# Every second load of a chunk split into 112, 8 and 8 partitions, in a hexagonal convolution with group norm

## The chip, the cores and the metric

The kernel runs on one core of a Trainium2 chip. The metric is the device time of one execution in microseconds. Three runs of the kernel before gave 752.25, 753.97 and 754.43 us; the median is 753.97 us. The profile is that of one more execution.

## The reference

`x` has shape (2048, 64, 16, 16) in float32: images, channels, rows, columns. What is computed is `x + conv(norm(x))`:

```
def _gn(v, G=32, eps=1e-5):           # pairs of channels of one image
    g = v.reshape(B_, G, C_ // G, H_, W_)
    return ((g - mean(g)) / sqrt(var(g) + eps)).reshape(v.shape)
...
xp = pad(x, 1); xp[:, :, DST_R, DST_C] = xp[:, :, SRC_R, SRC_C]      # 30 wrapped border pixels
up, left, right = conv4x4(xp, w_* masked to 5 taps, stride 2) + b_*
out[0::2, 0::2] = up; out[1::2, 0::2] = left; out[1::2, 1::2] = right
return x + out * OUT_MASK
```

## The kernel before

The 2048 images are taken in 64 chunks of 32 (`NCHUNK`). A chunk stands in SBUF as 128 partitions (64 channels of the even images, 64 of the odd ones) of 16 images of 256 pixels, 16 KB per partition, 2 MB in all. `xs` has eight slots for chunks (`SLOTS`); chunk k is in slot k modulo 8. It is loaded there, added to in place and stored from there.

What each engine does with chunk k:

- SP issues all transfers from one queue, in an order written out by hand (lines 177 to 209). The first chunk comes in four pieces (L179), then come the weights (L182, 64 partitions of 4 KB each), loads of chunks 1 and 2 (L169), six tiny biases (L188) and further loads up to chunk 6. After that it alternates: the store of chunk k (L175), which waits for `bank_added`, then the load of chunk k + 7 (L169), which waits until the store of chunk k - 1, which had the same slot, has landed (`stored`).
- DVE computes the statistics of chunk k + 1 (`bn`, L224, eight instructions) between the small steps that turn those of chunk k into a scale and a shift (L232 to L267), and then normalises eight of the 16 images into `tn` (L272). Before the first `bn` of a chunk it waits for the semaphore `loaded` of the slot (L221).
- ACT takes the square root (L305), normalises the other eight images (L311) and copies the finished PSUM banks of chunk k - 2 to `res`, with the bias (L340).
- POOL adds `res` to the slot (L395) and copies the wrapped border pixels in `tn` (L406).
- PE does the five taps of each of the three kernels as matmuls on 64 x 64 quarters (L451).

A load of 128 partitions is spread over 16 transfer engines, and `loaded[s]` rises by 16 when all have finished. A load's rows are 1 KB (one image of one channel), so it has 2048 of them.

Of the kernel before, what the change touches and what calls it, by code (L numbers as in the profile page):

```python
# [13 lines left out]
P = 128  # L14
B, C, HW = 2048, 64, 16
PIX = HW * HW
G = 16
NCHUNK = B // (2 * G)
SLOTS = 8
# [42 lines left out]


QUARTER = G // 4


WRAPS = [
# [14 lines left out]
def view(tensor, at, dims, first=0, parts=P):  # L82

    full = tensor[:, ]
    row = full.ap[0][0]
    return bass.AP(full.tensor, full.offset + first * row + at, [[row, parts]] + [list(d) for d in dims])


def hex_conv(nc, x, w_up, b_up, w_left, b_left, w_right, b_right, out):
    ctx = ExitStack()  # L90
    with ctx:
        def sb(name, shape, dt):
            return ctx.enter_context(nc.sbuf_tensor(name, shape, dt))

        def sem(name):
            return ctx.enter_context(nc.semaphore(name))

        x_dram = x.rearrange("(n g h) c r q -> n (h c) g (r q)", g=G, h=2)
        out_dram = out.rearrange("(n g h) c r q -> n (h c) g (r q)", g=G, h=2)

        xs = sb("xs", [P, SLOTS, G * PIX], F32)
# [26 lines left out]
        loaded = [sem(f"loaded{s}") for s in range(SLOTS)]  # L128
# [36 lines left out]
        @block.sync  # L165
        def _(sp):
            def load(k):
                s = k % SLOTS
                sp.dma_start(xs[:, s, :].rearrange("p (g q) -> p g q", g=G), x_dram[k]).then_inc(loaded[s], 16)  # L169

            def store(k):

                s = k % SLOTS
                sp.wait_ge(bank_added, NB * (k + 1))
                sp.dma_start(out_dram[k], xs[:, s, :].rearrange("p (g q) -> p g q", g=G)).then_inc(stored[s], 16)  # L175

            for n in range(4):
                pairs = slice(QUARTER * n, QUARTER * (n + 1))
                sp.dma_start(xs[:, 0, :].rearrange("p (g q) -> p g q", g=G)[:, pairs],  # L179
                             x_dram[0][:, pairs]).then_inc(quarter[n] if n < 3 else loaded[0], 16)  # L180
            for t, w in enumerate((w_up, w_left, w_right)):
                sp.dma_start(raw[:, t * C * 16:(t + 1) * C * 16],  # L182
                             w.rearrange("o c a b -> o (c a b)")).then_inc(w_loaded, 16)
            load(1)
            load(2)
            for t, b in enumerate((b_up, b_left, b_right)):
                for h in range(2):
                    sp.dma_start(bias[C * h:C * h + C, t:t + 1],  # L188
                                 b.rearrange("(o a) -> o a", a=1)).then_inc(b_loaded, 16)

            for k in range(3, SLOTS - 2):
                load(k)

            sp.wait_ge(bank_empty, PREP_BANKS)
            load(SLOTS - 2)

            for k in range(NCHUNK - 1):
                store(k)
                if k == 0:
                    load(SLOTS - 1)  # L200
                elif k + SLOTS - 1 < NCHUNK:
                    sp.wait_ge(stored[(k - 1) % SLOTS], 16 * ((k - 1) // SLOTS + 1))
                    load(k + SLOTS - 1)
            for half in range(2):
                pairs = slice(G // 2 * half, G // 2 * (half + 1))
                sp.wait_ge(bank_added, NB * (NCHUNK + half))
                sp.dma_start(out_dram[NCHUNK - 1][:, pairs],
                             xs[:, SLOTS - 1, :].rearrange("p (g q) -> p g q", g=G)[:, pairs]
                             ).then_inc(stored[SLOTS - 1], 16)
            for s in range(SLOTS):  # L210
                sp.wait_ge(stored[s], 16 * (NCHUNK // SLOTS + (s == SLOTS - 1)))

        @block.vector
        def _(dve):
            def bn(k, u0, u1):

                if k >= NCHUNK:
                    return
                s = k % SLOTS
                if u0 == 0 and k:  # L220
                    dve.wait_ge(loaded[s], 16 * (k // SLOTS + 1))  # L221
                for u in range(u0, u1):
                    both = view(xs, (s * G + 2 * u) * PIX, [(1, PIX), (PIX, 2)])
                    last = nc.vector.bn_stats(stats[:, k % 2, 2 * u:2 * u + 2].rearrange("p g a -> p (g a)"), both)  # L224
                if u1 == G // 2:
                    last.then_inc(bn_done, 1)

            def moments(k, ahead):

                done = STAT_OPS * k  # L230
                own = stats[:, k % 2]
                nc.vector.stream_shuffle(mate[:].rearrange("p g a -> p (g a)"), own.rearrange("p g a -> p (g a)"),  # L232
                                         [p ^ 1 for p in range(32)]).then_inc(stat_step, 1)
                bn(ahead, 0, 1)
                dve.wait_ge(stat_step, done + 1)
                nc.vector.tensor_tensor(gap[:], own[:, :, 1], mate[:, :, 1], ALU.subtract).then_inc(stat_step, 1)  # L236
                nc.vector.tensor_tensor(m2[:], own[:, :, 2], mate[:, :, 2], ALU.add).then_inc(stat_step, 1)  # L237
                nc.vector.tensor_tensor(msum[:], own[:, :, 1], mate[:, :, 1], ALU.add).then_inc(stat_step, 1)  # L238
                dve.wait_ge(stat_step, done + 2)
                nc.vector.scalar_tensor_tensor(gap2[:], gap[:], float(PIX // 2), gap[:],  # L240
                                               op0=ALU.mult, op1=ALU.mult).then_inc(stat_step, 1)
                bn(ahead, 1, 2)
                dve.wait_ge(stat_step, done + 5)

                nc.vector.scalar_tensor_tensor(var[:], gap2[:], EPS * GROUP, m2[:],  # L245
                                               op0=ALU.add, op1=ALU.add).then_inc(var_ready, 1)
                bn(ahead, 2, 4)
# [33 lines left out]
            for n in range(4):  # L281
                if n < 3:
                    dve.wait_ge(quarter[n], 16)
                else:
                    dve.wait_ge(loaded[0], 16)
                bn(0, QUARTER // 2 * n, QUARTER // 2 * (n + 1))
            dve.wait_ge(bn_done, 1)
# [222 lines left out]
```

## Time and profile before

| | |
|---|---|
| median of three runs | 753.97 us |
| lowest, highest | 752.25, 754.43 us |
| the profiled execution, its own time | 753.31 us |
| its span | 751.4 us |
| mean granted clock of TensorE | 0.991 |
| moved by the transfer engines | 269.68 MB, mean 359 GB/s |
| read from and written to HBM | 135.01 MB, 134.22 MB |

The span is the time from the first to the last instruction of the profile. An engine's busy share counts its instructions, without those that issue transfers or wait. The DMA share is the sum of the times of all packets over 16 engines' time; packets overlap a little on an engine, so it can stand above 1. The page's chain goes back from the last instruction, at each step to what released it.

### The profile page before, as it was taken

How to read it: one execution, taken by the hardware profiler on the slowest of the kernel's cores; microseconds unless marked ns; L12 is line 12 of the kernel's file. 1: busy time of each engine (PE TensorE's matmuls, PEld its weight loads, DVE VectorE, ACT ScalarE, POOL GpSimd, SP SyncE). 2: the span in 40 equal slices, each digit the busy share in tenths (PEclk: the TensorE clock that was granted, in tenths of full speed). 3: DMA queues.
4: the chain of work that ended last, by engine and by line, in shares of the span. 5: the costliest groups of instructions: out<-in, count | busy, mean ns of one | idle time of the engine just before them, and what ended most of it. 6: DMA issues, size and time to landing. Idle time of an engine off the chain costs nothing.

```text
span 751.4 us, 36371 instructions
## 1 busy us (share of the span) xinstructions
PE 662.4 (88%) x15697; PEld 610.1 (81%) x15697; DVE 668.0 (89%) x1793; ACT 579.5 (77%) x1258; POOL 488.1 (65%) x1115
## 2 busy tenths in 40 slices
PE   0889999999998898898898898898898898898874
PEld 0879999999998787887787887887887887887874
DVE  4899999999989999999989999999999999999910
ACT  1678889888887787787787787787787787787863
POOL 1077777777667667667667577577577676677673
PEclk9999999999999999999999999999999999999997
DMA  9999999999999999999999999999999999999984
GB/s 240 326 358 374 380 376 378 371 367 365 354 372 372 367 377 371 374 380 363 373 361 376 371 377 372 366 379 365 372 375 368 376 374 376 367 379 370 360 297 136
DMA packets 265022, 269.68 MB, mean 359 GB/s; under 512 B 2640, under 2 KB 264784, under 8 KB 264976
## 3 DMA queue, kind: packets, MB, share of 16 engines
q1 hardware_dynamic: 264976, 269.23, 104.6%
q14 instruction: 37, 0.30, 0.1%
q8 instruction: 9, 0.15, 0.1%
HBM read 135.01 MB, written 134.22 MB: 358 GB/s over the span
## 4 chain that ended last, share of the span: by engine, by line
DMA 66%; DVE 19%; PE 5%; ACT 3%; issue 3%; POOL 2%; SPq 1%; POOLq 0%; ACTq 0%
DMA xs<-in_x 41%; DMA out<-xs 25%; DVE stats L224 9%; DVE tn L272 5%; PE bank L451 5%; ACT tn L311 2%; POOL xs L395 2%; ACT res L340 1%; DVE small L256 1%; DVE small L260 1%; SPq L175 1%; DVE rstd L263 1%; POOL tn L406 1%; DVE nmr L267 1%; DVE m L237 0%
## 5 line engine op out<-in xcount | busy, mean ns | idle before, releaser
L451 PE MATMUL bank<-tn,wts 64*64 64x192 f32 (+5 forms) x15600 | 649.8, 323 | 9.1 <-issue 9.1
L451 PEld LDWEIGHTS bank<-tn,wts 64*64 64x64 f32 x15600 | 597.0, 137 | 42.3 <-issue 9.7
L395 POOL TENSOR_TENSOR xs<-res,xs 128x192 f32<-128x192 f32 (+6 forms) x780 | 388.5, 538 | 78.2 <-ACT res L340 77.7
L224 DVE BATCH_NORM_STATS2 stats<-xs 128x6 f32<-128x512 f32 x512 | 346.9, 690 | 45.4 <-DMA xs<-in_x 45.4
L340 ACT ACTIVATE res<-bank,bias 64x512 f32<-64x512 f32 (+6 forms) x650 | 304.6, 469 | 30.4 <-PE bank L451 20.6
L311 ACT ACTIVATE tn<-xs,nmr,rstd 128x256 f32<-128x256 f32 x511 | 258.9, 591 | 8.2 <-DVE nmr L267 6.7
L406 POOL COPY tn<-tn 128x128 f32<-128x128 f32 (+2 forms) x320 | 97.5, 360 | 179.5 <-ACT tn L311 179.5
L272 DVE TENSOR_SCALAR tn<-xs,rstd,nmr 128x256 f32<-128x256 f32 x513 | 198.6, 457 | 2.3
L305 ACT ACTIVATE std<-var 128x16 f32<-128x16 f32 x64 | 13.8, 215 | 123.8 <-DVE var L245 123.8
L462 PEld LDWEIGHTS bank<-blank 128*128 128x128 f16 x65 | 6.2, 96 | 70.5 <-issue 65.9
L462 PE MATMUL bank<-blank 128*128 128x2 f16 x65 | 11.4, 176 | 51.6 <-POOL tn L406 50.7
L256 DVE SCALAR_TENSOR_TENSOR small<-var,small 128x16 f32<-128x16 f32 x64 | 30.0, 468 | 0.1
L263 DVE SCALAR_TENSOR_TENSOR rstd<-small 128x16 f32<-128x16 f32 x64 | 28.5, 445 | 0.1
L430 PE MATMUL bank<-ident,xs 64*128 64x64 f32 x32 | 7.1, 419 | 19.9 <-ACT xs L353 19.9
L430 PEld LDWEIGHTS bank<-ident,xs 64*128 64x128 f32 x32 | 6.9, 329 | 19.9 <-ACT xs L353 19.9
L267 DVE SCALAR_TENSOR_TENSOR nmr<-msum,rstd 128x16 f32<-128x16 f32 x64 | 22.7, 354 | 0.1
L237 DVE TENSOR_TENSOR m<-stats,mate 128x16 f32<-128x16 f32 x64 | 21.2, 331 | 0.0
L238 DVE TENSOR_TENSOR msum<-stats,mate 128x16 f32<-128x16 f32 x64 | 19.8, 310 | 0.0
L240 DVE SCALAR_TENSOR_TENSOR gap<-gap 128x16 f32<-128x16 f32 x64 | 16.2, 252 | 0.0
L260 DVE TENSOR_TENSOR small<-small 128x16 f32<-128x16 f32 x64 | 15.7, 245 | 0.1
L253 DVE RECIPROCAL small<-std 128x16 f32<-128x16 f32 x64 | 14.8, 231 | 0.7 <-ACT std L305 0.7
L236 DVE TENSOR_TENSOR gap<-stats,mate 128x16 f32<-128x16 f32 x64 | 13.5, 211 | 0.1
(18 smaller groups left out, 36.3 us busy)
## 6 DMA issues: line engine op xcount, KB each, us to landing
xs<-in_x SPq DMA_DIRECT2D x63, 2048.0 KB, 16.8
out<-xs SPq DMA_DIRECT2D x63, 2048.0 KB, 17.0
xs<-in_x SPq DMA_DIRECT2D x4, 512.0 KB, 6.4
out<-xs SPq DMA_DIRECT2D x2, 1024.0 KB, 5.2
xs<-in_L_conv_w_up SPq DMA_DIRECT2D x1, 256.0 KB, 8.4
xs<-in_L_conv_w_left SPq DMA_DIRECT2D x1, 256.0 KB, 9.3
xs<-in_L_conv_w_right SPq DMA_DIRECT2D x1, 256.0 KB, 12.6
bias<-in_L_conv_b_up SPq DMA_DIRECT2D x2, 0.2 KB, 7.3
```

Of the source, the lines that this page charges most:

```text
L224: last = nc.vector.bn_stats(stats[:, k % 2, 2 * u:2 * u + 2].rearrange("p g a -> p (g a)"), both)
L237: nc.vector.tensor_tensor(m2[:], own[:, :, 2], mate[:, :, 2], ALU.add).then_inc(stat_step, 1)
L256: nc.vector.scalar_tensor_tensor(small[:, 1], var[:], -0.5 / GROUP, small[:, 0], op0=ALU.mult, op1=ALU.mult).then_inc(stat_step, 1)
L260: nc.vector.tensor_tensor(small[:, 2], small[:, 1], small[:, 0], ALU.mult).then_inc(stat_step, 1)
L263: nc.vector.scalar_tensor_tensor(rstd[:], small[:, 2], 1.5, small[:, 0], op0=ALU.add, op1=ALU.mult).then_inc(stat_step, 1)
L267: nc.vector.scalar_tensor_tensor(nmr[:], msum[:], -0.5, rstd[:], op0=ALU.mult, op1=ALU.mult).then_inc(norm_ready, 1)
L272: last = nc.vector.tensor_scalar(t_image(b, g), x_image(s, g), rstd[:, g:g + 1], nmr[:, g:g + 1], ALU.mult, ALU.add)
L311: last = nc.scalar.activation(t_image(k % 2, g), x_image(k % SLOTS, g), ACT.Identity, bias=nmr[:, g:g + 1], scale=rstd[:, g:g + 1])
L340: last = nc.scalar.activation(res[onto, BANK_AT[j] + at:BANK_AT[j] + at + cols], psum[NB * b + j][banks, at:at + cols], ACT.Identity, bias ...
L395: last = nc.gpsimd.tensor_tensor(onto, view(res, at, [(rows * w, pairs), (w, rows), (1, w)]), onto, ALU.add)
L406: last = nc.gpsimd.tensor_copy(view(tn[b], dst, [(T_PAIR, G)] + [(d, n) for d, _, n in dims]), view(tn[b], src, [(T_PAIR, G)] + [(d, n) fo ...
L451: last = nc.tensor.matmul(psum[bank + j][to:to + C, at:at + cols], wts[first:first + C, NT * rect[0] + n, :], taps(b, rect, tap, g0, pairs ...
```

## The change

Loads into the odd slots (1, 3, 5 and 7, so those of the odd chunks) are issued as three transfers: partitions 0 to 111, 112 to 119 and 120 to 127. By its author's count the first gives seven partitions to each of the 16 transfer engines, and each of the other two gives one to each of the lower eight, so that the lower eight carry nine partitions and the upper eight seven. All three raise the slot's semaphore by 16, and DVE waits for three times 16 there. Loads into even slots, the first chunk and all stores are unchanged.

```diff
 QUARTER = G // 4
+SPLIT = (((0, P),), ((0, 112), (112, 120), (120, P)))
...
             def load(k):
                 s = k % SLOTS
-                sp.dma_start(xs[:, s, :].rearrange("p (g q) -> p g q", g=G), x_dram[k]).then_inc(loaded[s], 16)
+                for p0, p1 in SPLIT[s % 2]:
+                    sp.dma_start(xs[p0:p1, s, :].rearrange("p (g q) -> p g q", g=G),
+                                 x_dram[k][p0:p1]).then_inc(loaded[s], 16)
...
                 if u0 == 0 and k:
-                    dve.wait_ge(loaded[s], 16 * (k // SLOTS + 1))
+                    dve.wait_ge(loaded[s], 16 * len(SPLIT[s % 2]) * (k // SLOTS + 1))
```

SP's queue around the first loads that follow a store, before the change (a row is a run of like instructions; `out<-xs` is a store, `xs<-in_x` a load, with partitions x images x pixels):

```order
L175 DMA out<-xs 128x16x256 [waits bank_added]
L169 DMA xs<-in_x 128x16x256
L175 DMA out<-xs 128x16x256 [waits bank_added]
L169 DMA xs<-in_x 128x16x256 [waits stored0]
L175 DMA out<-xs 128x16x256 [waits bank_added]
L169 DMA xs<-in_x 128x16x256 [waits stored1]
```

The same place with the change:

```order
L178 DMA out<-xs 128x16x256 [waits bank_added]
L171 DMA xs<-in_x 112x16x256
L171 DMA xs<-in_x 8x16x256 x2
L178 DMA out<-xs 128x16x256 [waits bank_added]
L171 DMA xs<-in_x 128x16x256 [waits stored0]
L178 DMA out<-xs 128x16x256 [waits bank_added]
L171 DMA xs<-in_x 112x16x256 [waits stored1]
L171 DMA xs<-in_x 8x16x256 x2
```

The loads of chunks 7 and 9 have become three issues each, the one of chunk 8 between them is as it was, and the order of chunks and waits is the same. The order of the other engines is unchanged.

## Rows read from the trace of the kernel before

**Rows 1.** The page, part 2: the span in 40 equal slices.

```profile
DMA  9999999999999999999999999999999999999984
GB/s 240 326 358 374 380 376 378 371 367 365 354 372 372 367 377 371 374 380 363 373 361 376 371 377 372 366 379 365 372 375 368 376 374 376 367 379 370 360 297 136
```

**Rows 2.** The page, parts 1 and 5: busy us and share; DVE's wait.

```profile
PE 662.4 (88%) x15697; PEld 610.1 (81%) x15697; DVE 668.0 (89%) x1793; ACT 579.5 (77%) x1258; POOL 488.1 (65%) x1115
...
L224 DVE BATCH_NORM_STATS2 stats<-xs 128x6 f32<-128x512 f32 x512 | 346.9, 690 | 45.4 <-DMA xs<-in_x 45.4
```

**Rows 3.** The page, part 4: the chain that ended last, by engine.

```profile
DMA 66%; DVE 19%; PE 5%; ACT 3%; issue 3%; POOL 2%; SPq 1%; POOLq 0%; ACTq 0%
```

**Rows 4.** The chain in order of time, middle: start us, us, what.

```profile
303.84 16.93 DMA out<-xs
320.78 16.74 DMA xs<-in_x
337.89 16.87 DMA out<-xs
354.77 16.76 DMA xs<-in_x
```

**Rows 5.** Timeline of SP, 378 to 406 us: start us, us, instruction.

```profile
378.11 5.43 SPq L169 DMA_DIRECT2D xs<-in_x  x1
383.59 5.45 SPq L175 DMA_DIRECT2D out<-xs  x1
389.09 5.71 SPq L169 DMA_DIRECT2D xs<-in_x  x1
394.85 5.31 SPq L175 DMA_DIRECT2D out<-xs  x1
400.24 5.54 SPq L169 DMA_DIRECT2D xs<-in_x  x1
```

**Rows 6.** Windows: length, busy us by engine, then PEclk, DMA share, GB/s.

```profile
65.00:110.00 45.00, 45.00 (x1064) 41.45 (x1058) 44.85 (x122) 39.91 (x87) 32.98 (x75) 1.00 1.09 378
110.00:187.00 77.00, 77.00 (x1858) 70.82 (x1854) 76.75 (x213) 67.27 (x144) 57.02 (x130) 1.00 1.07 370
188.00:278.00 90.00, 83.79 (x1995) 77.63 (x1991) 83.65 (x228) 71.84 (x155) 61.30 (x138) 1.00 1.07 368
278.00:368.00 90.00, 81.18 (x1932) 74.41 (x1928) 84.71 (x224) 70.81 (x152) 60.12 (x137) 1.00 1.07 372
548.00:638.00 90.00, 80.92 (x1927) 74.43 (x1922) 84.61 (x225) 70.96 (x152) 60.41 (x137) 1.00 1.07 374
```

**Rows 7.** The page, part 6: issues, KB each, us to landing.

```profile
xs<-in_x SPq DMA_DIRECT2D x63, 2048.0 KB, 16.8
out<-xs SPq DMA_DIRECT2D x63, 2048.0 KB, 17.0
```

**Rows 8.** The chain in order of time, early: first and last of eleven like pieces.

```profile
75.49 3.39 DVE tn L272 x8
...
178.33 2.85 DVE tn L272 x8
```

**Rows 9.** Timeline of SP, 2 to 16 us: the issues of the weights.

```profile
2.88 0.55 SPq L182 DMA_DIRECT2D xs<-in_L_conv_w_up  x1
3.47 0.63 SPq L182 DMA_DIRECT2D xs<-in_L_conv_w_left  x1
4.14 0.60 SPq L182 DMA_DIRECT2D xs<-in_L_conv_w_right  x1
```

**Rows 10.** Windows of 1 us around the weights' transfers, columns as in rows 6.

```profile
3.00:4.00 1.00, 0.00 (x0) 0.00 (x0) 0.00 (x0) 0.20 (x1) 0.27 (x2) 1.00 1.08 380
...
10.00:11.00 1.00, 0.00 (x0) 0.00 (x0) 0.86 (x2) 0.00 (x0) 0.00 (x0) 1.00 1.02 182
11.00:12.00 1.00, 0.00 (x0) 0.00 (x0) 0.43 (x1) 0.00 (x0) 0.00 (x0) 1.00 1.02 184
12.00:13.00 1.00, 0.00 (x0) 0.00 (x0) 0.00 (x0) 0.00 (x0) 0.00 (x0) 1.00 1.07 186
...
18.00:19.00 1.00, 0.00 (x0) 0.00 (x0) 1.00 (x5) 1.00 (x7) 0.00 (x0) 1.00 1.11 350
```

## The prediction

> **What bounds the kernel now.** I began with the 40 slices of the page. The DMA row stands at nine tenths in 38 of 40 slices, while no compute engine is full [rows 1]: PE is busy for 88% of the span, DVE for 89%, ACT for 77%, POOL for 65% [rows 2]. The chain that ended last puts 66% of the span on transfers and 19% on DVE [rows 3]. In the chain's middle part one load or store follows the other, each some 16.8 us from issue to landing [rows 4].
>
> That landing time isn't the cost of a transfer, for several are in flight. The cost shows in SP's own rows: SP is held 5.3 to 5.7 us in each issue, load and store alike, because the queue takes the next only as room comes free [rows 5]. The windows say the same: from 188 to 706 us the engines move 368 to 374 GB/s at a DMA share of 1.07 [rows 6]. A chunk is 128 x 4096 x 4 B = 2.10 MB, so a transfer costs 2.10 MB / 372 GB/s = **5.64 us**, and a chunk (a load and a store) 11.3 us. There are 63 loads and 63 stores of this size [rows 7], and the first chunk and the last store in pieces: 128 x 5.64 = 722 us of a span of 751.4 us.
>
> DVE is the next limit. Between 75.49 and 178.33 us, where chunks wait ready in the eight slots, the chain runs on DVE and ten chunks take 102.8 us, so 10.3 us each [rows 8]. Even there the transfers run at 370 to 378 GB/s [rows 6]. So whatever lengthens a transfer on its busiest engine lengthens the kernel, and DVE's 1 us a chunk is the most that faster transfers could give back. Afterwards DVE waits for loads 45.4 us in all [rows 2].
>
> **The change, part by part.** All durations are of one profiled execution, which took 753.31 us (span 751.4); the median of the runs shown is 753.97, so the sum is made on 753.31 and differs from the median by 0.1%.
>
> *SP's issues.* 32 of the 63 large loads (odd chunks, 1 to 63) become three issues. The 64 added ones cost SP about 0.6 us each, by the issues of the weights, the nearest ones into a queue that is not yet full [rows 9]: 38 us in all. I cost them at nothing: SP stands 5.5 us in each issue because the transfers are slow, and its issues run ahead of the data by 16.8 - 5.6 = 11 us. If that cover went, it would be 1.2 us for every second chunk. What stands behind the longer load on SP is the next store, and behind it the next load; both only fill the queue.
>
> *DVE's wait.* It waits for 48 instead of 16 in the odd slots. It costs nothing itself, but it now ends with the last of three transfers, thus with the lower eight transfer engines. Behind it on DVE stand the statistics, then the normalisation, then PE.
>
> *The share of each engine.* A whole load is eight partitions per engine in 5.64 us, so 0.705 us per partition (16 rows of 1 KB). The upper eight now have seven: 4.94 us. The lower eight have 7 + 1 + 1: were each partition as cheap as now, 6.35 us. Over a load and a store of both kinds the lower eight have 33 partitions for 32, the upper eight 31.
>
> *The two small pieces.* Here the price is open. The trace has only three transfers that reach less than 128 partitions and are not tiny: the weights, 64 partitions each. While they move, the rate falls to 182 to 186 GB/s, and the DMA share stays at 1.02 to 1.07; the whole loads around them run at 350 to 380 GB/s [rows 10]. So all engines are busy, and every packet takes 1.9 times as long. My reading: the way into the partitions of SBUF is what is shared, and with half of the partitions two engines press on the same entry. The small pieces are a sixteenth of the partitions for eight engines. Bounds: factor f = 1 (no such sharing at this size) to f = 8 (all eight engines behind one entry). In between, f = 2 is what the 64 partitions show, and f = 4 is two entries for eight engines, if neighbouring partitions lie behind the same one. I take 4, midway in doublings between the measured 2 and the worst 8, since eight neighbours are much narrower than 64.
>
> The Trainium skill, SBUF — State Buffer, section "Door 1: The DMA port swizzle", speaks against this change: four neighbouring partitions share one of 16 ports, and it gives 27.6 GB/s for partitions 0 to 3 alone. By that the eight partitions of a piece reach two ports, an estimate of 131 KB / 55.2 GB/s = 2.4 us a piece, and the sum would end near 883 us. The trace agrees as far as it goes: 64 partitions gave 183 of 350 GB/s.
>
> *Sum.* On the lower eight a split load takes 7 x 0.705 + 2 x f x 0.705 us. Against 5.64 that adds (2f - 1) x 0.705: with f = 4, 4.94 us. The stores and the even loads stay as they are. All of it lies on the path, since the transfers are the bound from end to end; it is added 32 times: 158 us. 753.3 + 158 = **911 us**. A pair of chunks takes 27.5 us instead of 22.6, DVE needs 20.6 of them.
>
> *What I leave out of the sum.* Cut by seven, the 112 partitions no longer fall on the engines in groups of eight, so neighbours behind one entry may belong to two engines. If two of an engine's seven partitions collide at double price, it adds 1.41 x 32 = 45 us. Against that, engines that drift apart don't press on the entry at once. I let the two cancel and keep both for the range.
>
> **The rivals.**
> - *f = 2 instead of 4*, since the eight engines get out of step or the entries are finer: (2 x 2 - 1) x 0.705 x 32 = 68 us, so 821 us. For it: it is the only factor measured. Against: eight engines start the pieces together, each with one partition.
> - *f = 8, one entry for all*: 15 x 0.705 x 32 = 338 us, 1092 us. For it: rate in proportion to partitions is one reading of 64 of 128. Against: it needs all eight neighbours behind one entry.
> - *No sharing, and an engine of the lower eight is the one that is late today*: it gets 33/32 of the work, 5.64 / 32 = 0.176 us for each of 128 transfers, 22.6 us: 776 us. For it: one slow engine holds the queue, and every whole transfer has the same share for each. Against: the rows of the weights.
> - *Faster: no sharing, and the engines that are late today are all in the upper eight.* Then 31/32 of their work is worth up to 22.6 us. The price is limited by the lower eight: they must move 33/32 in less than 5.64 us, thus do 5.64 x 32/33 = 5.47 us for today's share, a rate of 383 GB/s. The best slice of the page shows 380 GB/s, 5.52 us [rows 1]. From 383 GB/s on this rival decides; halfway to its 22.6 us it gives 743 us. For it: between 65 and 110 us the queue ran at 378 GB/s, later at 372, so something falls behind later. Against: the rows name no engine, and the small pieces must be free of the cost above. On this the Trainium skill, DMA: Bandwidth & Descriptors, section "Latency and other measured facts", says that engines 7 and 15 are usually the slow ones, one of each half, though for another issue path. By it the lower one would bind and the time be that of the rival before; no row here shows it.
> - *Nothing changes*: an engine's share is no limit because the memory is. Then 753 us. Against: the rate rises to 378 to 380 in stretches.
>
> **How the numbers follow.** Forecast f = 4: 0.55. f = 2: 0.18. f = 8: 0.05. No sharing, lower engine late: 0.08. Faster rival: 0.10. Nothing: 0.04. The predicted time is that of the likeliest, 911 us; its own range is 830 (much of the pressing lost by drift, half of the 158 us) to 956 (with the 45 us). The range of the whole goes down to 770, so that f = 2 (821) and the late lower engine (776) are in it, and up to 970, the 956 with a little room. It leaves out the faster rival, the unchanged case and f = 8, 0.19 in all. About 0.3% is what a measurement of this kernel can tell from no change. Faster by more: 0.10. Within: 0.04, which I round up to 0.05. Slower: 0.85.
>
> **What the profile of the changed kernel would show.** If I am right: the windows of the middle fall from 372 to about 300 GB/s, with a DMA share that falls less than the rate, because packets of the small pieces take several times as long; the time from issue to landing of the 8-partition loads is far over that of their 16 rows; DVE's wait for loads grows from 45 to over 150 us; PE and DVE keep their busy times. If the no-sharing readings hold, the rate stays within 3% of 372 GB/s. I'm wrong in kind if the rate in the middle stays at 370 or above, and wrong in size only if it falls to 340 (f = 2) or under 260 (f = 8).

## The result and the profile after

The changed kernel takes **846.33 us** (843.21 to 849.38, four runs) against 753.24 us for the kernel before in the same comparison: a ratio of **1.124** (95% interval 1.121 to 1.128), so 93 us more. Forecast were 911 us, within 770 to 970. The direction and the place are right, the size is 59% of the forecast one, and the experiments show that one term of the sum was far too large and another was left out. Where the runs of one kernel lie over 1.5% apart, the slower ones are left out of its time and ratio below.

The page after, parts 1, 2, 4 and 5, in the lines that answer to [rows 1 to 3]:

```profile
PE 701.8 (83%) x15697; PEld 636.4 (75%) x15697; DVE 647.4 (76%) x1793; ACT 579.9 (68%) x1258; POOL 488.4 (58%) x1115
...
DMA  9999999999999999999999999999999999999985
GB/s 215 226 216 304 330 347 320 327 329 336 333 343 329 323 321 336 333 351 333 328 315 335 324 356 339 319 321 340 328 348 328 327 322 333 329 343 342 321 286 196
...
DMA 55%; SPq 17%; DVE 11%; POOL 8%; PE 3%; ACT 3%; issue 2%; ACTq 0%; POOLq 0%
...
L227 DVE BATCH_NORM_STATS2 stats<-xs 128x6 f32<-128x512 f32 x512 | 347.1, 691 | 162.3 <-DMA xs<-in_x 162.1
```

The transfer engines are as full as before and move less. DVE waits 162 us for loads, where it waited 45. Of the windows, the whole middle first, then nine single microseconds around one split load (columns as in [rows 6]):

```profile
188.00:638.00 450.00, 384.84 (x8548) 347.74 (x8546) 362.89 (x1002) 317.30 (x679) 270.15 (x606) 0.92 1.06 332
...
408.00:409.00 1.00, 1.00 (x28) 0.76 (x24) 1.00 (x3) 0.96 (x4) 1.00 (x4) 1.00 1.12 210
409.00:410.00 1.00, 1.00 (x30) 0.99 (x25) 0.96 (x4) 0.97 (x3) 1.00 (x4) 1.00 1.10 205
410.00:411.00 1.00, 1.00 (x32) 0.99 (x28) 1.00 (x4) 1.00 (x3) 1.00 (x3) 1.00 1.12 205
411.00:412.00 1.00, 1.00 (x36) 1.00 (x31) 1.00 (x4) 1.00 (x3) 0.04 (x1) 1.00 1.08 325
412.00:413.00 1.00, 1.00 (x45) 1.00 (x42) 0.29 (x3) 1.00 (x3) 0.00 (x0) 1.00 1.10 386
...
415.00:416.00 1.00, 0.96 (x15) 0.80 (x19) 0.00 (x0) 0.00 (x0) 0.00 (x0) 1.00 1.08 375
416.00:417.00 1.00, 1.00 (x21) 0.84 (x17) 0.91 (x5) 0.00 (x0) 0.00 (x0) 1.00 0.87 274
417.00:418.00 1.00, 1.00 (x22) 0.91 (x18) 1.00 (x5) 0.11 (x1) 0.00 (x0) 1.00 0.92 308
418.00:419.00 1.00, 1.00 (x24) 0.95 (x20) 1.00 (x3) 0.97 (x3) 0.27 (x1) 1.00 1.03 359
```

The middle runs at 332 GB/s, where it ran at 368 to 374 [rows 6]. That is 8.39 MB / 332 GB/s = 25.3 us for a pair of chunks instead of 22.6. Two things happen within a pair. From 408 to 411 us the engines are fully busy (share 1.10 to 1.12) at 205 to 210 GB/s, a full share at a low rate, as with the weights in [rows 10]. From 416 to 418 us the share itself falls, to 0.87 and 0.92: some engines have nothing to do. In this pair the first is the larger part. Which transfer makes which is counted at the end of the experiments.

SP's timeline in the same stretch:

```profile
408.24 7.41 SPq L171 DMA_DIRECT2D xs<-in_x  x1
415.69 6.43 SPq L178 DMA_DIRECT2D out<-xs  x1
422.16 10.75 SPq L171 DMA_DIRECT2D xs<-in_x  x3
432.95 0.90 SPq L178 DMA_DIRECT2D out<-xs  x1
433.89 7.53 SPq L171 DMA_DIRECT2D xs<-in_x  x1
```

A pair takes 25.65 us here. The three issues of a split load hold SP for 10.75 us, no longer 5.5 [rows 5]; it is still the queue that holds it.

### The profile page after: what moved, and what is told of

It is laid out like the page before. It is cut to its first block, busy times and chain, and to the rows that moved or that the text cites. A ratio compares the mean times of both kernels' runs of the same rounds, so it can differ in the third digit from the quotient of the medians.

```text
span 847.4 us, 36435 instructions
## 1 busy us (share of the span) xinstructions
PE 701.8 (83%) x15697; PEld 636.4 (75%) x15697; DVE 647.4 (76%) x1793; ACT 579.9 (68%) x1258; POOL 488.4 (58%) x1115
## 4 chain that ended last, share of the span: by engine, by line
DMA 55%; SPq 17%; DVE 11%; POOL 8%; PE 3%; ACT 3%; issue 2%; ACTq 0%; POOLq 0%
DMA xs<-in_x 50%; SPq L171 13%; POOL xs L398 8%; DVE stats L227 6%; DMA out<-xs 5%; PE bank L454 3%; ACT res L343 2%; SPq L178 2%; DVE tn L275 1%; SPq L191 1%; DVE m L240 1%; DVE msum L241 1%; DVE gap L239 1%; ACT tn L314 0%; DVE gap L243 0%
## 5 line engine op out<-in xcount | busy, mean ns | idle before, releaser
L454 PE MATMUL bank<-tn,wts 64*64 64x192 f32 (+6 forms) x15600 | 688.7, 335 | 7.2 <-issue 7.2
L454 PEld LDWEIGHTS bank<-tn,wts 64*64 64x64 f32 x15600 | 623.1, 143 | 53.2 <-issue 7.8
L240 DVE TENSOR_TENSOR m<-stats,mate 128x16 f32<-128x16 f32 x64 | 16.7, 261 | 0.0
L241 DVE TENSOR_TENSOR msum<-stats,mate 128x16 f32<-128x16 f32 x64 | 13.9, 217 | 0.0
L235 DVE STREAM_SHUFFLE mate<-stats 128x48 f32<-128x48 f32 x64 | 12.8, 200 | 0.0
L243 DVE SCALAR_TENSOR_TENSOR gap<-gap 128x16 f32<-128x16 f32 x64 | 12.3, 193 | 0.0
```

Of the source, the lines that this page charges most:

```text
L454: last = nc.tensor.matmul(psum[bank + j][to:to + C, at:at + cols], wts[first:first + C, NT * rect[0] + n, :], taps(b, rect, tap, g0, pairs ...
```

## Experiments

One partition of a load costs an engine 0.705 us, its plain share; f is the factor by which a small piece costs more. Which partition goes to which engine is the count of the change's author; no row of a trace names an engine. The question was which of the three new features costs: the small pieces of neighbouring partitions (theory 1, the prediction's), the 112 partitions, which are cut by sevens (theory 2), or the nine for eight shares on the lower engines (theory 3).

**Each shape alone.** The kernel holds nothing but lines of this form, 14 shapes, six transfers each (shortened):

```diff
+            def alone(make):
+                for i in range(6):
+                    make(i)
+                    n += 1
+                    sp.wait_ge(done, 16 * n)
...
+            alone(lambda i: sp.dma_start(slot(i), x_dram[...]).then_inc(done, 16))
+            alone(lambda i: sp.dma_start(slot(i)[0:112], x_dram[...][0:112]).then_inc(done, 16))
...
+            alone(lambda i: sp.dma_start(slot(i)[0:32:4], x_dram[...][0:32:4]).then_inc(done, 16))
```

> No convolution at all: SP issues one transfer at a time and waits until it has landed, six times for each of 14 shapes (whole; partitions 0-111; 16-127; 112-119; 120-127; eight partitions in steps of four; 112-127; 0-63; 0-95; 14 of 16 images; 0-111 and whole from memory in which each partition's 16 KB are contiguous; a whole store; a store of 0-111). Read is the time from issue to landing. Theory 1 (the prediction's: the 8-partition pieces are dear, four engines press on one entry of SBUF, the 112 are cheap): a piece of eight neighbours takes about 2.1 us longer than one in steps of four, and 0-111 takes 0.7 us less than whole. Theory 2 (the 112 partitions are dear, since cut by sevens they put two engines on one entry, and the pieces are cheap): neighbours and steps of four within 1 us of each other, 0-111 takes about 1.5 to 2 us more than whole. 14 images (the same bytes as 112 partitions, cut by eights) 0.7 us less than whole in both. If 0-111 from contiguous memory is as slow as 0-111, it is SBUF's side; if it is fast, the memory's.

The view of one line's instructions. After the count stand the least, median and greatest ns of the issue, then the starts of the first and the last of six in us; a fifth of their distance is the time of one transfer with its wait.

```profile
L116 SPq DMA_DIRECT2D xs<-in_x x6: 367/368/449, 0.7 to 41.7; - x6
L117 SPq DMA_DIRECT2D xs<-in_x x6: 313/313/339, 49.8 to 98.7; - x6
L118 SPq DMA_DIRECT2D xs<-in_x x6: 312/313/313, 108.1 to 156.0; - x6
L119 SPq DMA_DIRECT2D xs<-in_x x6: 272/273/324, 165.4 to 185.1; - x6
L120 SPq DMA_DIRECT2D xs<-in_x x6: 272/273/273, 188.9 to 208.9; - x6
L121 SPq DMA_DIRECT2D xs<-in_x x6: 677/677/855, 212.7 to 228.0; - x6
L122 SPq DMA_DIRECT2D xs<-in_x x6: 312/312/328, 231.1 to 251.9; - x6
L123 SPq DMA_DIRECT2D xs<-in_x x6: 596/596/705, 255.9 to 292.5; - x6
L124 SPq DMA_DIRECT2D xs<-in_x x6: 312/313/319, 299.8 to 347.0; - x6
L125 SPq DMA_DIRECT2D xs<-in_x x6: 368/368/390, 356.4 to 393.8; - x6
L126 SPq DMA_DIRECT2D xs<-in_x x6: 312/312/343, 401.2 to 449.8; - x6
L127 SPq DMA_DIRECT2D xs<-in_x x6: 327/328/353, 459.2 to 498.7; - x6
L128 SPq DMA_DIRECT2D out<-xs x6: 372/373/399, 506.4 to 544.0; - x6
L129 SPq DMA_DIRECT2D out<-xs x6: 317/318/344, 551.5 to 591.1; - x6
```

| shape | us each |
|---|---|
| whole (L116) | 8.2 |
| partitions 0-111 (L117), 16-127 (L118) | 9.8, 9.6 |
| 14 of 16 images, the same bytes (L125) | 7.5 |
| 0-63 (L123), 0-95 (L124) | 7.3, 9.4 |
| eight neighbours (L119, L120) | 3.9, 4.0 |
| eight in steps of four (L121) | 3.1 |
| sixteen neighbours (L122) | 4.2 |
| contiguous memory: 0-111 (L126), whole (L127) | 9.7, 7.9 |
| store: whole (L128), 0-111 (L129) | 7.5, 7.9 |

These times hold the issue and the wait too. From the first packet of a transfer to the end of its last, the trace has 6.6 to 6.7 us for the whole load, 5.7 to 6.1 for 14 images, 7.7 to 8.7 for 0-111, 5.0 to 5.4 for 0-63, 1.7 to 1.9 for eight neighbours and 1.2 to 1.4 for eight in steps of four. (The 6.6 and 5.2 us in the expectation for two halves, below, are such times.)

The table has theory 2's numbers. A transfer of 0-111 takes 1.6 us longer than one with more bytes and 2.3 us longer than one with the same bytes. It isn't the memory's side, for with contiguous memory it is 9.7 us against 7.9. It isn't the number of bytes, and not which 112 partitions. What is left is which partitions move, and how they fall on the engines; these two are not told apart. 96 partitions (six each) are nearly as slow as 112. Eight neighbours cost 0.9 us more than eight in steps of four by this table and 0.5 us more by their packets, where f = 4 would have been 2.1.

**112 and 16.** `SPLIT = (((0, P),), ((0, 112), (112, P)))`.

> Odd loads as 112 and 16 partitions: every engine again carries eight (7 + 1). Theory 1 (small neighbouring pieces dear, f = 4, and the 112 at their share): 4.94 + 2.82 us against 5.64, so 32 x 2.1 = 68 us over before, 821 us. Theory 2 (the 112 dear at about 7.3 us, pieces cheap): 32 x (7.3 + 0.7 - 5.64) = 75 us, 828 us, little under the change's 846. Theory 3 (what costs is that the lower eight carry more): back to 753 us.

831.9 us in the faster of two runs that lie wide apart (the other took 853.9), 79 us over the kernel before. It can't separate theories 1 and 2, but it ends theory 3 as the main cause: with eight shares on every engine the time doesn't come back to 753 us. It is more than 112 partitions cost by the 1.5 us a load found below, 48 us; the rest is not explained by the parts.

**Small pieces without the 112.**

```diff
                 sp.dma_start(xs[:, s, :]...
+                if s % 2 and k > SLOTS:
+                    for p0, p1, st in ((112, 120, 1), (120, 128, 1)):
+                        sp.dma_start(spare[p0:p1:st, :]..., x_dram[k][p0:p1:st]).then_inc(spared, 16)
```

Ahead of such a load SP also waits for the pair before; the trace shows no time spent in that wait.

> All loads whole as before; from chunk 9 on every odd load is followed by two more loads of 8 partitions (112-119 and 120-127) into a spare buffer that nobody reads: 28 pairs of small pieces without any 112-partition transfer. Theory 1 (f = 4): 28 x 2 x 2.82 = 158 us, 911 us. Theory 2 (f = 1, only their own packets on the lower eight): 28 x 1.41 = 39 us or less, at most 793 us.

800.9 us (ratio 1.065, 1.054 to 1.076): 48 us for 28 pairs, 1.7 us a pair. Their plain share is 1.41 us, so f is 1.2 in the stream (1.0 to 1.4 by the interval), and the time is 8 us over theory 2's bound. Theory 1 asked for 911 us. **It falls.**

**The same, in steps of four:** `((0, 32, 4), (64, 96, 4))` in the place of the two ranges.

> As k2_spare_small (801 us), but each small piece has eight partitions in steps of four (0, 4, ... 28 and 64, 68, ... 92) instead of eight neighbours; same bytes, same lower eight engines. If the neighbours' pressing on one entry still costs in the stream: 28 x 2 x up to 0.8 us (the difference of the two alone) less than k2_spare_small, 760 to 790 us. If it is hidden there and only the pieces' own packets count: about 800 us again.

794.8 us (ratio 1.056, 1.046 to 1.067), 1.5 us a pair. The neighbours' extra of 0.9 us each, seen when alone, would be 50 us; it is mostly gone, and the 6 us between the two kernels are within their intervals.

**112 partitions without the small pieces.**

```diff
+                n = 112 if s % 2 and k >= SLOTS else P
-                sp.dma_start(xs[:, s, :]..., x_dram[k]).then_inc(loaded[s], 16)
+                sp.dma_start(xs[0:n, s, :]..., x_dram[k][0:n]).then_inc(loaded[s], 16)
```

> Odd loads from chunk 9 on bring partitions 0-111 alone, one transfer each; partitions 112-127 of the slot keep what stood there (this part of the input is left out). Theory 1 (112 at their share): 28 x 0.7 = 20 us less than before, 733 us. Theory 2 (112 dear at 7.3 us): 28 x 1.7 = 47 us more, 800 us.

776.9 us (ratio 1.033, 1.020 to 1.046), 24 us more for an eighth fewer bytes in 28 loads. Theory 2 had the sign, but said 47 us. With the small pieces beside the 112 (827.5 us, below) it is 50.6 us more again, 1.8 us a pair: there too f = 4 would have been 5.6.

**Its control, 14 images:** `n = 14 if s % 2 and k >= SLOTS else G`, and `[:, 0:n]` on both sides.

> The control of k3_only112: odd loads from chunk 9 on bring 14 of the 16 images for all 128 partitions, the same 1792 KB, but cut by eights (two images of the input are left out). If the cut by sevens is what cost k3_only112 its 24 us: 28 x 0.7 = 20 us less than before, 733 us. If a smaller transfer just doesn't pay in this queue: 753 us or more.

735.1 us (ratio 0.977, 0.972 to 0.982), where 733 were expected. The middle window of the control and, in the second fence, that of the 112:

```profile
188.00:638.00 450.00, 419.88 (x10017) 386.75 (x10009) 424.45 (x1155) 365.87 (x782) 311.31 (x699) 1.00 1.07 369
```

```profile
188.00:638.00 450.00, 396.99 (x9269) 364.08 (x9262) 385.25 (x1074) 341.06 (x729) 289.15 (x651) 0.98 1.09 345
```

Same bytes, same number of transfers, share full in both; 369 against 345 GB/s. Loading 112 partitions costs (776.9 - 735.1) / 28 = **1.5 us a load**, 1.1 to 1.9 with the intervals. Single microseconds of the kernel with 112 show the loss, without any small piece in it:

```profile
408.00:409.00 1.00, 1.00 (x21) 0.91 (x16) 1.00 (x4) 0.96 (x3) 1.00 (x3) 1.00 1.11 348
409.00:410.00 1.00, 1.00 (x26) 0.96 (x21) 1.00 (x3) 0.96 (x3) 1.00 (x2) 1.00 1.12 222
410.00:411.00 1.00, 1.00 (x30) 1.00 (x26) 1.00 (x3) 0.97 (x3) 1.00 (x3) 1.00 1.13 195
...
413.00:414.00 1.00, 1.00 (x46) 1.00 (x41) 1.00 (x4) 1.00 (x3) 0.58 (x2) 1.00 1.09 241
414.00:415.00 1.00, 1.00 (x43) 1.00 (x36) 0.83 (x5) 1.00 (x3) 0.00 (x0) 1.00 1.09 381
```

**All loads by sevens:** `n = 112 if k >= SLOTS else P`.

> All loads from chunk 8 on bring partitions 0-111 alone: twice the dose of k3_only112 (777 us; the rest of the input is left out). If the cut costs the same each time: 753 + 56 x 0.87 = 802 us. If two in a row let the engines drift apart and the pressing is lost: under 790 us.

808.6 us (ratio 1.073, 1.066 to 1.081): 55 us for 56 loads, 0.99 us each beside 0.87 for every second one. The cost goes with the dose and doesn't get lost by drift (802 were expected for that, under 790 for the other).

**Nine and seven without anything else.** 14 images whole plus two pieces in steps of four:

```diff
+                n = 14 if s % 2 and k > SLOTS else G
+                sp.dma_start(xs[:, s, :]...[:, 0:n], x_dram[k][:, 0:n]).then_inc(loaded[s], 16)
+                ... for p0, p1, st in ((0, 32, 4), (64, 96, 4)): (to the spare buffer, as above)
```

> The redistribution by itself, without a cut by sevens and without neighbours: odd loads from chunk 9 on bring 14 images for all 128 partitions (seven shares per engine), and two pieces of eight partitions in steps of four into a spare buffer (one share each on the lower eight): nine and seven, the bytes of before (two images of the input are left out). If the lower eight have room and the late engines are upper ones: under 750 us. If a transfer is as long as its busiest engine: 753 + 28 x 0.7 = 773 us. If the issues themselves or the idle upper engines cost more: over 775 us.

771.6 us (ratio 1.026, 1.019 to 1.032): 19 us / 28 = **0.69 us a load**, a full share of 0.705. The eight engines that get the pieces have no room, so the redistribution the change is about costs even when it is done without 112 partitions and without neighbours. The faster rival falls by this run.

**Two halves:** `SPLIT = (((0, P),), ((0, 64), (64, P)))`.

> All odd loads as two halves, partitions 0-63 and 64-127, on all 16 engines: eight partitions per engine, no small piece, no cut by sevens. If engines that write to the same half of the partitions share entries two by two (alone, 64 partitions took 5.2 us for half of the bytes, a whole load 6.6): 32 x (2 x 5.2 - 6.6) = 122 us more, 875 us. If only the cut or the small pieces matter: 753 us.

865.9 us (ratio 1.151, 1.145 to 1.156), where 875 were expected: 114 us / 32 = 3.5 us a load. Every engine has its eight partitions, no piece is small, and with the kernel of small pieces first (865.0, below) it is the slowest split of all. That two engines of one half share an entry of SBUF is the plainest reading, but a reading: the middle has a share of 1.09 at 322 GB/s, and no row shows an entry.

```profile
188.00:638.00 450.00, 379.86 (x8342) 342.37 (x8336) 344.51 (x967) 308.00 (x659) 262.43 (x589) 0.89 1.09 322
```

**The change's three transfers, small ones to the spare buffer.** Both edits above together.

> Partitions 0-111 to the slot, 112-119 and 120-127 to the spare buffer, in the odd loads from chunk 9 on: the change's three transfers in 28 loads instead of 32, and the link between its time and the parts measured so far (the slot's upper 16 partitions keep what stood there). If the parts add up (cut by sevens 1.5 us, nine for eight 0.7 us, neighbours 0.2 us): 753 + 28 x 2.4 = 820 us. If they work on each other as in the change (93 us / 32 = 2.9 us a load): 834 us.

827.5 us (818.9 to 829.6; ratio 1.096, 1.089 to 1.103), 74 us / 28 = 2.65 us a load, between the two expectations. 112 partitions (1.5) and redistribution (0.7) give 2.2; 0.5 us a load is left that the parts don't explain. The intervals of the kernels in this sum add up to about as much, so the rest is barely clear of noise.

**The same in steps of four.**

> As the kernel with 112 partitions and two neighbouring spare pieces, but the two pieces have their eight partitions in steps of four. If the neighbours are cheap in the stream (0.2 us): 6 us under that kernel. If what the parts don't explain comes from the neighbours beside the 112 partitions: 14 to 20 us under it, about 814 us.

828.5 us (817.9 to 829.6; ratio 1.093, 1.084 to 1.103): no difference. So the rest doesn't come from neighbours either.

**Small pieces first:** `SPLIT = (((0, P),), ((112, 120), (120, P), (0, 112)))`.

> The change with the two small pieces issued ahead of the 112 partitions. If each transfer costs what it costs by its shape: 846 us again. If the rest (about 16 us) comes from small pieces that run beside the next store while the upper eight wait for work: the order matters, and the time moves by over 5 us.

865.0 us (862.9 to 868.0; ratio 1.147, 1.144 to 1.150), 19 us more than the change for the same three shapes. The order matters. Windows of this kernel around one split load:

```profile
410.00:411.00 1.00, 0.29 (x5) 0.29 (x9) 1.00 (x5) 0.00 (x0) 0.57 (x3) 1.00 1.05 374
411.00:412.00 1.00, 1.00 (x20) 0.85 (x19) 1.00 (x4) 0.59 (x2) 0.00 (x0) 1.00 0.74 231
412.00:413.00 1.00, 1.00 (x16) 0.85 (x11) 1.00 (x3) 0.96 (x3) 0.74 (x1) 0.51 0.91 282
413.00:414.00 1.00, 1.00 (x15) 0.86 (x11) 1.00 (x3) 0.97 (x2) 1.00 (x3) 0.50 1.05 350
414.00:415.00 1.00, 1.00 (x18) 0.88 (x14) 1.00 (x4) 0.96 (x3) 1.00 (x3) 0.50 1.13 244
415.00:416.00 1.00, 1.00 (x24) 0.87 (x20) 1.00 (x4) 0.96 (x4) 1.00 (x3) 0.78 1.11 238
416.00:417.00 1.00, 1.00 (x30) 0.97 (x26) 0.96 (x3) 0.96 (x4) 1.00 (x3) 1.00 1.12 250
417.00:418.00 1.00, 1.00 (x34) 1.00 (x29) 1.00 (x4) 1.00 (x4) 1.00 (x4) 1.00 1.13 228
418.00:419.00 1.00, 1.00 (x37) 1.00 (x31) 1.00 (x4) 1.00 (x4) 0.29 (x1) 1.00 1.11 206
419.00:420.00 1.00, 1.00 (x45) 1.00 (x40) 0.54 (x4) 1.00 (x4) 0.00 (x0) 1.00 1.12 242
```

Again there is a hole (share 0.74) and a slow stretch at full share, here six microseconds. One pair says little, so all 450 single microseconds from 188 to 638 us were counted in each profile:

| kernel | DMA share 1.00 or more, under 250 GB/s | DMA share under 1.00 |
|---|---|---|
| before | 0 | 20 |
| the change | 60 | 57 |
| small pieces first | 101 | 42 |
| 112 partitions, every second load | 81 | 0 |
| 112 partitions, every load | 123 | 7 |
| two halves of 64 | 127 | 3 |
| 14 images | 1 | 18 |
| 14 images and spare pieces in steps of four | 1 | 54 |
| whole, and spare pieces: neighbours; steps of four | 3; 0 | 57; 59 |
| 112 partitions and spare pieces: neighbours; steps of four | 68; 57 | 37; 55 |

The slow stretches stand only where loads of 112 or 64 partitions run, and small pieces alone make none. The holes go beyond the 18 to 20 of the kernels without pieces only where pieces give eight engines more than the others. So the larger of the two things in the profile after is the 112 partitions' and the smaller the redistribution's. With the small pieces first it is the slow stretches that grow, while the holes, which the expectation had in mind, get fewer. That engines entering the 112 at different times press on each other longer would fit this, and may be the 0.5 us of the change too; no run here shows it by itself, so it stays open.

## Why the prediction was right, and where its size was wrong

**What bounds the kernel: right.** One share more on eight engines lengthened the kernel by 0.69 us a load (k6_nine_seven), and k4_14images, with one share less on every engine, came out at 735 us where 733 were worked out.

**SP's added issues at nothing: as far as can be seen, right.** k6_nine_seven has the same number of added issues in its 28 loads and costs no more than the share of the lower eight.

**Nine for eight, 0.705 us: right**, measured 0.69 (0.51 to 0.87 with the interval).

**The small pieces, f = 4: the step that failed.** The rows of the weights [rows 10] were read rightly (half of the partitions, half of the rate at a full share; k5_64_64 agrees), but carried to the wrong transfer. Forecast were 2 x 4 x 0.705 = 5.6 us a load for the two pieces. Measured are 1.5 to 1.7 beside whole loads and 1.8 beside the 112, so f is 1.1 to 1.3. On this the Trainium skill, SBUF — State Buffer, section "Door 1: The DMA port swizzle", gives four neighbouring partitions one port, an estimate of 2.4 us a piece; alone, a piece took 3.9 us with its fixed part, against 3.1 in steps of four (1.7 to 1.9 and 1.2 to 1.4 by the packets), and in the stream the difference was not to be told from nothing. The measurement decides.

**What was left out of the sum: the main term.** The text named it, two of an engine's seven partitions at double price, 1.41 us a load, and let it cancel against a drift that k9b_all112 doesn't show. Measured is 1.5 us. The price agrees; that it is two of seven at double price is not shown by it.

**The sum with measured terms.** The 112 partitions 1.49, the redistribution 0.69, and the rest, which is what k10b_112_spare_small has over these two, 0.47: 2.65 us a load. The middle of the change agrees and is measured apart from them: 25.3 - 22.6 = 2.7 us a pair. Of the 32 split loads three (chunks 1, 3 and 5) are issued before 63 us, where loads follow loads and no store lies between. There a split load costs more. The first 63 us of the kernel before, then of the changed one, then of k10b_112_spare_small, which splits from chunk 9 on:

```profile
0.00:63.00 63.00, 39.54 (x740) 36.63 (x742) 49.45 (x138) 36.37 (x92) 22.32 (x61) 0.97 1.03 314
```

```profile
0.00:63.00 63.00, 33.73 (x549) 30.15 (x553) 39.60 (x112) 29.27 (x77) 16.35 (x48) 0.92 1.04 220
```

```profile
0.00:63.00 63.00, 39.72 (x735) 36.33 (x739) 49.27 (x139) 36.36 (x92) 22.73 (x62) 0.97 1.03 313
```

(314 - 220) x 63 / 372 = 16 us are lost here, over 5 us a split load; why they are dearer at the start no run tells. 29 x 2.65 + 16 = 93 us, as measured. The forecast's 32 x 4.94 had too dear a piece and left out the price of the 112, and two errors of opposite sign made it come out nearer than it deserved: that 846 us lie in its range is in part luck. With pieces at their measured 1.7 us and nothing else changed its sum would have been 32 x 1.0 = 32 us, a third of what was measured.

**The rivals.** "f = 2" gave 821 us, nearer than the forecast, but for another reason. The faster rival, with its point at 383 GB/s, falls by k6_nine_seven: the engines with the pieces have no room. (Its own terms give 742 us, not 743, and half of the 158 us gives 832 for the lower end, not 830.) The late lower engine at 776 us was right about the redistribution (0.69 us in 28 loads) and saw nothing of the cut. f = 8 and "nothing changes" fall.

**What the profile was to show.** The rate of the middle was put at 300 GB/s for f = 4 and 340 for f = 2; it is 332. DVE's wait over 150 us: 162. The share was to fall less than the rate: it went from 1.07 to 1.06. The landing of the 8-partition loads was to be late; the page gives no landing for them. PE and DVE were to keep their busy times: DVE's went from 668 to 647 us, PE's from 662 to 702, while the granted clock of the middle fell from 1.00 to 0.92. In the windows of the last kernel PE was busy for 0.29 of the microsecond from 410, and from 412 to 415 its clock stands at 0.50 to 0.51 (the 1.2 GHz level). It isn't on the path there: the transfers are full.

## What to carry to other kernels

Keep a large load on all 128 partitions, and if less must be moved, take fewer columns, not fewer partitions: 14 images gave 2.3% of the kernel back, 112 partitions took 3.3%. Before shifting work between transfer engines, test whether the receiving ones have room, with a piece into a spare buffer. And read the DMA share together with the rate: here a full share at a low rate came with loads on fewer partitions, a share under 1 with pieces that only some engines had.

## What the runs showed of the hardware

- Alone, loads of 96 and of 112 partitions take longer (9.4 and 9.8 us) than one of 128 (8.2 us); stores suffer less (7.9 against 7.5 us).
- In a full queue of loads and stores, a load of 112 partitions costs 1.5 us more than one of 128 with the same bytes, and two halves of 64 cost 3.5 us more than the whole.
- Eight partitions alone cost 3.1 us in steps of four and 3.9 us as neighbours, yet issuing the stepped ones holds SP for 0.68 us, the neighbours for 0.27. Partitions 0-63 took 0.60 us to issue, the other loads 0.31 to 0.37.
- The same three transfers, 32 times, differ by 19 us with their order (846 and 865 us).
- The times of the kernels with loads of 112 partitions spread by 0.6 to 2.6% (843.2 to 849.4 us for the change, 831.9 to 853.9 with 112 and 16), those of the kernel before by 0.4%.
